# The front of a graph network kernel: all of x normalised before the first counting tile, a cast moved to ACT, two memsets released early

## What is computed

```python
h = relu(layernorm(x))
# three SAGE convolutions; agg = segment mean over incoming edges
h1 = relu(mean(h[src]) @ Wl1.T + bl1 + h @ Wr1.T)
h2 = relu(mean(h1[src]) @ Wl2.T + bl2 + h1 @ Wr2.T) + h1
x = x + mean(h2[src]) @ Wl3.T + bl3 + h2 @ Wr3.T
# one message-passing layer
h = relu(layernorm(x))
msg = silu(concat(h[src], edge_attr) @ mw1 + mb1)
x = x + h + silu(concat(h, segment_sum(msg, dst)) @ uw1 + ub1) @ uw2 + ub2
```

## Time and profile before

| | |
|---|---|
| median of 3 runs | 2412.69 us (2410.21 to 2415.8) |
| profiled execution, its own time | 2419.6 us |
| span of the profiled execution | 2417.8 us |
| PE busy | 2165.6 us, 90% |
| POOL busy | 1698.0 us, 70% |
| DVE busy | 1180.9 us, 49% |
| ACT busy | 677.9 us, 28% |
| first counting tile on PE | 77.65 us |
| first gather issued | 122.48 us |
| block 0 summed (tick 78) | 151.81 us |

### The profile page before, as it was taken

How to read it: one execution, slowest core, us unless ns; L and a number is a source line. 1 busy time by engine, 2 the same in 40 slices (tenths; PEclk the granted TensorE clock), 3 DMA queues, 4 the chain that set the end, 5 groups by cost and what they waited for, 6 DMA issues and landing times.

```text
span 2417.8 us, 45832 instructions
## 1 busy us (share of the span) xinstructions
PE 2165.6 (90%) x14802; PEld 1347.8 (56%) x14802; DVE 1180.9 (49%) x3931; ACT 677.9 (28%) x1218; POOL 1698.0 (70%) x1735
## 2 busy tenths in 40 slices
PE   0489999999799999999999968999999999999988
PEld 0235554444344444445555546777777777777766
DVE  8877888777411111522333344444444444444443
ACT  3777776666400000200011132111111111111111
POOL 4377777777277777377777537777777777777775
PEclk9679999999999999999999976989999899999998
DMA  4289999998589898588888644444444444444442
GB/s 115 96 286 295 310 308 299 287 297 287 184 260 271 270 269 261 162 263 270 257 262 249 187 154 129 113 113 114 119 112 116 122 114 112 117 119 120 113 115 55
DMA packets 329384, 465.39 MB, mean 192 GB/s; under 512 B 36484, under 2 KB 278055, under 8 KB 322487
## 3 DMA queue, kind: packets, MB, share of 16 engines
q1 hardware_dynamic: 255656, 263.83, 37.5%
q0 software_dynamic: 66288, 135.86, 19.5%
q10 hardware_dynamic: 7200, 62.72, 6.6%
HBM read 378.63 MB, written 83.64 MB: 191 GB/s over the span
## 4 chain that ended last, share of the span: by engine, by line
PE 36%; POOL 28%; issue 10%; DVE 2%; DMA 1%; ACT 1%; POOLq 0%; DVEq 0%; SPq 0%
POOL gath L767 28%; PE bank L1046 25%; PE bank L1093 2%; PE bank L1005 2%; PE bank L1070 1%; PE bank L1002 1%; PE bank L1251 1%; PE bank L1252 1%; PE bank L1135 1%; DMA gath<-table,src_sb 1%; PE bank L1108 0%; PE bank L1021 0%; POOL parts L701 0%; PE bank L1109 0%; DMA shared<-in_x 0%
## 5 line engine op out<-in xcount | busy, mean ns | idle before, releaser
L767 POOL DMA_INDIRECT gath<-table,src_sb x1641 | 1604.7, 978 | 552.8 <-issue 527.0
L1046 PE MATMUL bank<-region,parts 128*128 128x500 f16 (+2 forms) x4116 | 952.5, 369 | 10.1 <-DVE dense_sum L1492 10.0
L1046 PEld LDWEIGHTS bank<-region,parts 128*128 128x128 bf16 x4116 | 360.3, 97 | 373.2 <-issue 20.2
L845 ACT CAST shared<-bank 128x490 f32 x600 | 373.8, 623 | 145.3 <-PE bank L1024 112.3
L1484 DVE TENSOR_TENSOR acc<-acc,bank 128x31 f32 (+1 forms) x564 | 108.8, 193 | 510.8 <-PE bank L1005 353.9
L1093 PE MATMUL bank<-shared,parts 128*128 128x384 bf16 x1890 | 353.4, 338 | 0.0
L1600 DVE TENSOR_TENSOR region<-bank,gath 128x384 f32<-128x384 f32 x260 | 144.7, 557 | 410.8 <-issue 227.9
L949 ACT ACTIVATE region<-region 128x384 f32<-128x384 f32 x260 | 135.8, 522 | 747.1 <-DVE region L1600 743.6
L1002 PE MATMUL bank<-onehot,region 128*128 128x31 f32 x1662 | 236.8, 281 | 81.7 <-ACT region L949 39.8
L1002 PEld LDWEIGHTS bank<-onehot,region 128*128 128x128 f32 x1662 | 240.0, 209 | 120.8 <-ACT region L949 100.7
L1070 PE MATMUL bank<-mw,region 128*128 128x128 f32 x1560 | 263.1, 311 | 0.7 <-DVE shared L1646 0.7
(11 more groups left out here) (165 smaller groups left out, 1367.5 us busy)
## 6 DMA issues: line engine op xcount, KB each, us to landing
region<-counts SPq DMA_DIRECT2D x234, 625.0 KB
counts<-shared ACTq DMA_DIRECT2D x50, 1225.0 KB
region<-in_edge_T SPq DMA_DIRECT2D x138, 384.0 KB, 3.3
gath<-table,src_sb POOLq DMA_INDIRECT x1641
region<-counts SPq DMA_DIRECT2D x35, 500.0 KB
table<-parts SPq DMA_DIRECT2D x36, 384.0 KB, 2.6
shared<-in_src_row SPq DMA_DIRECT2D x17, 192.0 KB, 3.7
acc<-in_x SPq DMA_DIRECT2D x12, 256.0 KB, 5.4
```

The source lines that it names most:

```text
L767: pool.indirect_dma_start(out=(gath if l == 3 else gath_parts)[:, BT * place + j, :], out_offset=None, in_=table[l], in_offset=bass.Indire ...
L845: counted = nc.scalar.copy(stage[:, g % 2, :, bass.ds(at, CW)], count_bank(t))
L1046: mm = nc.tensor.matmul(sum_bank(ordinal)[:, 0:g * G].rearrange("p (b n) -> p b n", b=g), parts[:, hi, a, :], ring[:, q, 0:g, h * G:(h + 1 ...
```

## The change

Five edits:

1. `AHEAD_CHUNKS` becomes 13, so all chunks start at negative ticks (from -78 on); no chunk is started between counting ticks. Of the last chunk only the first part, the second part and the turned copy fall into ticks 0, 3 and 4, and PE's turn into tick 1.
2. The cast of the first destinations leaves DVE; ACT does it at its third negative tick, behind the square root of chunk 0.
3. POOL no longer waits for `edges_in` ahead of its two memsets. The wait stands behind them.
4. DVE writes the second group of low rows behind the first six pair rows and no longer in front of them.
5. A constant, `STARTS_AT`, places edit 2.

```diff
--- before.py
+++ after.py
@@ -142,9 +142,10 @@
         yield i, range(n0, n), range(steps_done(l, i - 1) if i else 0, steps_done(l, i))
 
 
-AHEAD_CHUNKS, CHUNK_TICKS = 9, 6
+AHEAD_CHUNKS, CHUNK_TICKS = 13, 6
 DEVIATION_AT, SCALE_AT, POSITIVE_AT, PART_AT, ROWS_TURN_AT, SECOND_AT, FEATURES_AT = 1, 3, 4, 6, 7, 9, 10
 LN_FROM = -AHEAD_CHUNKS * CHUNK_TICKS
+STARTS_AT = 2
 PREPARED_AT, COUNT_LEFT_AT, TAKE_LEFT_AT, FIRST_HOTS_AT, FLAG_AT = 30, 32, 40, 42, 52
 
 
@@ -731,9 +732,9 @@
                             in_offset=bass.IndirectOffsetOnAxis(ap=idx_left[:, 0:1].bitcast(U32), axis=0),
                         ).then_inc(s["gathered"], 16)
 
-            pool.wait_ge(edges_in, 64)
             nc.gpsimd.memset(shared[:, :].bitcast(F32), 0.0).then_inc(starts_ready, 1)
             nc.gpsimd.memset(acc[:, 0, :], 0.0).then_inc(acc_zeroed, NCH)
+            pool.wait_ge(edges_in, 64)
             for l in range(4):
                 if l == 0:
                     staggered((1, third_part(st[0], rest_rows)), (0, first_rest(st[0], kept_rows, rest_rows)))
@@ -820,6 +821,9 @@
                     features(st[0], "turned", 0)(c, c % 2, JC if c < NCH - 1 else JL)
 
             for i in range(LN_FROM, 0):
+                if i == LN_FROM + STARTS_AT:
+                    act.wait_ge(edges_in, 64)
+                    nc.scalar.copy(start_f[:, 0:NC], first_i[:, 0:NC]).then_inc(starts_step, 1)
                 normalise_chunks(i)
             act.wait_ge(consts_in, 16 * 11)
 
@@ -1319,7 +1323,6 @@
 
                 dve.wait_ge(edges_in, 64)
                 nc.vector.memset(start_f[:, NC:NC + 2], FAR)
-                nc.vector.tensor_copy(start_f[:, 0:NC], first_i[:, 0:NC]).then_inc(starts_step, 1)
                 by_group = start_f[:, 0:NC].rearrange("p (g t) -> p g t", t=GT)
                 for t in range(1, GT):
                     here, before = by_group[:, :, t:t + 1], by_group[:, :, t - 1:t]
@@ -1535,10 +1538,10 @@
                     m.then_inc(degree_hot_ready, 1)
 
                 if l == 0:
-                    for b in range(2):
-                        low_hot(b)
+                    low_hot(0)
                     for t in range(NPAIR - 1):
                         pair_hot(t)
+                    low_hot(1)
                 else:
                     for n in range(HOTS if l < 3 else 0):
                         hot(n)
```

## The result

| | before | after |
|---|---|---|
| median | 2413.58 us (6 runs, 2410.21 to 2415.8) | 2422.57 us (6 runs, 2422.09 to 2425.11) |
| ratio | | 1.004, 95% interval 1.003 to 1.0051 |
| profiled execution, span | 2417.8 us | 2420.8 us |

The change costs 9.0 us, 7.2 to 12.3 by the interval. 4.2 were forecast, as no change that a measurement can tell, and the measured median lies 0.6 us above the range. The spans of the two profiles differ by only 3.0 us. Why the medians differ by 6 us more than the profiles turned out to be the main question.

A forecast was written before the change was run, and what follows sets the result against it. The prediction took PE's count of tile 78, where POOL's gather ring opens, as the anchor bounding the kernel. Its terms -5.0 + 17.7 - 8.5 = +4.2 us gave 2416.9 us against the median (+0.17%), range 2408 to 2422.

The forecast's parts named there:

- term 1: Start of the front: with memsets early and the cast moved to ACT, DVE's scan starts at 14.7, not 19.66: -5.0 us.
- Term 2: Front ahead of tick 0: four more chunks at 4.42 us each, with nothing to hide them: +17.7 us.
- Term 3: Counting ticks, from DVE's low rows to PE's tile 78: less chunk work, faster ACT copies, a memset in full: -8.5 us.
- The one-to-one passage: From PE's count of tile 78 to the kernel's end: any shift of that instant reaches the end in full.
- The ring: POOL's seven gather places: full until PE counts tile 78, so earlier gathers gain nothing; POOL idles some 25 us.
- F: Theory formed after the result: the kernel's time moves one to one with PE's count of tile 78.
- L: Theory formed after the result: something behind PE's count of tile 78 costs several us, some 7.
- The small cast: Rival at the start: DVE's small cast beats POOL's memsets, scan at 10.5, -9.15; sum 0.0, 2412.7 us; chance 0.15.
- The slower rival: Counting ticks: stores and copies keep 9.1 us per 12 tiles; +6.4, 2419.1 us; chance 0.2.
- ACT alone: Rival in the counting ticks: ACT's copies set the pace at 0.623 us per tile; -1.6, 2411.1 us; chance 0.15.
- The head start: Rival on POOL's gathers: starting 20 us ahead saves PE's 6.86 us wait near layer 0's end; 2410 us; chance 0.1.

The follow-up runs named there:

- g_held: Kernel before, with DVE's wide cast made to wait until both of POOL's memsets are done: 2419.06 us against 2413.76, ratio 1.0021.
- f_before: Kernel before, unchanged, run and profiled again on one of the slow chips: 3030.56 us, ratio 0.9988.
- g_dose: Kernel before, with 48 DVE memsets of 480 columns, each waited for, ahead of the first low rows: 2442.82 us against 2413.76, ratio 1.0114.
- h_ahead13: Kernel before with only AHEAD_CHUNKS raised from 9 to 13: 2425.43 us against 2411.85, ratio 1.0049.
- h_rest9: Changed kernel with AHEAD_CHUNKS back at 9, all other edits kept: 2411.56 us against 2411.85 for the kernel before, ratio 1.0002.
- g_best: Changed kernel with 9 chunks ahead and POOL's memsets waiting for DVE's two small casts: 2410.55 us, ratio 0.9981 to the kernel before.
- i_first8: Kernel before with POOL's memsets waiting for DVE's wide cast and AHEAD_CHUNKS at 8: 2411.41 us against 2415.28, ratio 0.9981.
- i_late: Changed kernel with POOL's layer 0 gathers held until 42 tiles are counted: 2424.83 us against 2415.28 for the kernel before, ratio 1.0035.
- h_afterfree: Changed kernel with POOL's memsets waiting for DVE's two small casts: 2418.78 us against 2411.85 for the kernel before, ratio 1.0025.
- g_first: Kernel before, with POOL's memsets made to wait for DVE's wide cast: 2409.40 us, ratio 0.9983.

## Why the prediction was wrong

**The base.** This is the step that failed: term 1, read from one execution and then set against the median. The prediction took "the memsets held it throughout" in one execution for what the kernel before does, and set term 1 against it. In six of seven profiles the cast gets in between the two memsets, and g_held, where it can't, takes 2419 where the kernel before takes 2413.8. Against the usual execution, with its scan at 14.0 (f_before, g_dose) the change gains 0.7 us at the scan, not 5. The warning stood in the text: the profiled execution lay 6.9 us above the median. The prediction only subtracted the 6.9 from the sum and did not ask where in the timeline they were; an operation that takes 9.87 us where 0.47 is normal was the plainest candidate. Before that subtraction its sum gave 2423.8, within 1.2 us of both the profiled execution and the median of the changed kernel.

**Term 1** had its mechanism right (the small cast is held, POOL is first, by 0.09 us) and its size off: the scan started at 13.4, not 14.7, mostly because the statistics of chunk 0 did not follow the held casts but ended with them, at 12.00. So -6.3 against the first profile where -5.0 was forecast.

**Term 2**, +17.7, was right: 17.7 in h_ahead13. DVE turned to the low rows at 84.9, where 87.2 was forecast: 1.3 of it is term 1, and 1.0 is gained during the preparation; h_rest9 has that 1.0 as well (from scan to low rows 53.8 us where before has 54.8), so it belongs to the start and not to the chunks.

**Term 3**, -8.5, was right: 77.4 became 68.6, -8.8. Its parts too: the pace of 8.63 us per 12 tiles was 8.7. The memset held DVE for some 4.6 us (an estimate: 5.05 for L1411, where a cast of 600 that nothing holds takes 0.47), in a preparation step and not in a pair row as the prediction had it.

**The one-to-one passage** of tick 78 was right as far as g_dose tests it. **The ring** was right: POOL idled 30 us where 25 were foreseen. A slip on which nothing hangs: the gather at 594.64 is not the last of layer 0 but the 345th of 351, so the gathers up to it are 441.5 / 323 = 1.37 us apart, not 1.34.

**The sum again**, against the usual execution of before: low rows 84.9 - 68.9 = +16.0, low rows to block 0 -8.8, together +7.2. Measured 9.0 (7.2 to 12.3). Some 2 us are left for what lies behind tick 78, within the interval for this one kernel.

The same excess shows in the other kernels with 13 chunks. Set block 0 of the usual execution of before at 68.9 + 77.4 = 146.3, an estimate, and take for every kernel of the table how much its median is over that of the kernel before on its chip, less how much its block 0 is later than 146.3. The five kernels with 13 chunks have 1.8 to 5.2 us left, the six with 9 or 8 have -0.6 to 1.4 (each time is known to some 2 or 3 us). So F alone is too low for all five, and L holds in part: with 13 chunks something behind tick 78 costs some 2 to 5 us. The profiles agree only in part: five with 9 chunks have 449.2 to 451.7 from block 0 to the last gather of layer 0, five with 13 have 452.2 to 453.7; but g_best and i_first8, with 453.9 and 454.6, have 9 and 8, in executions 5.7 and 2.7 us above their medians. What it is **stays open**. The early gathers are a candidate that i_late does not exclude, and single profiles scatter behind block 0 by as much as is looked for.

**The rivals.** The small cast did not get in first: in all eight profiles with the early memsets and no added wait it was held. Where it was made first, in h_afterfree, the scan started at 10.39, as that rival had it (10.5). The slower rival came nearest to the measured time (2419.1 forecast) by luck: its reason was wrong, the stores came every 8.7 us. ACT alone did not set the pace. The head start counted nothing. No rival asked whether the base was typical, and that was the one that was needed.

**The rule on two inputs.** The Trainium skill ("SBUF — State Buffer", "Who interferes with whom") has a DVE instruction with two SBUF inputs run freely beside a GpSimd instruction that only writes. g_best and g_first agree: scan operations of 0.25 us beside the memsets, as elsewhere. Of a DVE instruction in a mode that uses two ports for one tensor, which a cast can enter, the same section of the Trainium skill says that whoever issues first gets the shared pair of ports for the whole instruction. No row shows the mode of the casts. Nor does that rule alone give what was seen: in nine profiles (one of the wide cast, eight of the small one) a cast recorded well ahead of POOL's second memset had to let that memset go first as well, where in six (all of the wide cast) it got in between. At the first memset the order can't be read from the rows of the wide cast, whose record starts 0.01 to 0.02 us ahead of the memset that it then waits for.

## What to carry to other kernels

Compare the profiled execution's own time with the median before any row is used, and if it lies apart by more than the effect looked for, find where, since that piece may be a race that usually goes the other way. Moving steps out of a loop that has room beside them into a front that has none costs their full latency (4.42 us per chunk here against 2.2 in the ticks, the mean of four), however much idler the loop then looks. A producer that is only allowed a ring ahead gains nothing from starting early.

## What the runs showed of the hardware that was not expected

- A cast on DVE that is ready while POOL writes with two memsets back to back either slips between them (4.52 us in all) or waits for both (9.87 us): 6 to 1 over seven profiles with the same code at this place, and both ways for the kernel before itself (f_before and the first profile). A small cast that became ready 0.09 us after the first memset's start was held through both in all eight profiles of that order.
- Behind held casts DVE's statistics, which read x alone, ended with the casts: the record shows them from 3.61 to 12.00, where the casts end too. They cost nothing on top.
- Two chips gave medians of about 3033 us for the kernel before and three others 2412 to 2415. Within their intervals the ratios of the same kernels agree: 1.0042 and 1.004 for the change, 1.0025 and 1.0042 against 1.0049 for thirteen chunks.
